# Softplus as one ScalarE function in a fused Mamba and feed-forward layer, its second half beside the silus of z

## The reference

```python
xi, z = split(x @ W_in.T)                       # 512 channels each
u  = silu(causal_conv4(xi) + conv_b)
dbl = u @ W_xproj.T                             # 16 ranks of dt, then B (16) and C (16)
dt = softplus(dbl[:, :16] @ W_dt.T + b_dt)      # what the change is about
h_t = exp(dt_t * A) * h_{t-1} + (dt_t * u_t) * B_t     # 512 channels x 16 states
y  = (h_t . C_t + u * D_skip) * silu(z)
x1 = layernorm(x + y @ W_out.T)
out = layernorm(x1 + (silu(x1 @ wg.T) * (x1 @ wu.T)) @ wd.T)
```

## Time and profile before

| | |
|---|---|
| median of 3 runs | 1799.51 us (1798.69 to 1802.62) |
| span of the profiled execution | 1797.7 us; the page gives no other time for it, and the median of the runs lies 1.8 us above this span |
| busy, share of the span | PE 96%, ACT 95%, DVE 93%, POOL 82% |
| granted TensorE clock, mean | 0.992 of full speed |
| DMA, share of 16 engines | under 20% |

### The profile page before, as it was taken

How to read it: one execution, slowest core, us unless ns; L and a number is a source line. 1 busy time by engine, 2 the same in 40 slices (tenths; PEclk the granted TensorE clock), 3 DMA queues, 4 the chain that set the end, 5 groups by cost and what they waited for, 6 DMA issues and landing times.

```text
span 1797.7 us, 40378 instructions
## 1 busy us (share of the span) xinstructions
PE 1734.7 (96%) x15678; PEld 1214.6 (68%) x15678; DVE 1675.1 (93%) x1970; ACT 1712.9 (95%) x2907; POOL 1477.8 (82%) x852
## 2 busy tenths in 40 slices
PE   7779999999999999999999999999999999999997
PEld 3456676767667676676767667676676767667676
DVE  5999999999999999999999999999999999999974
ACT  6999999999999999999999999999999999999971
POOL 5897987979889797997979889797987979889850
PEclk9999999999999999999999999999999999999999
DMA  7040211304013030211304013040311304022000
GB/s 211 1 121 1 56 65 15 118 11 121 3 16 118 15 118 2 66 68 16 118 10 123 2 15 119 14 119 1 74 60 16 118 13 121 1 39 83 1 25 24
DMA packets 171487, 100.57 MB, mean 56 GB/s; under 512 B 139408, under 2 KB 157584, under 8 KB 163232
## 3 DMA queue, kind: packets, MB, share of 16 engines
q1 hardware_dynamic: 171296, 97.98, 19.3%
HBM read 88.52 MB, written 9.44 MB: 54 GB/s over the span
## 4 chain that ended last, share of the span: by engine, by line
PE 48%; ACT 26%; DVE 11%; issue 9%; POOL 5%; SPq 0%; DMA 0%; ACTq 0%; POOLq 0%; DVEq 0%
PE ring L1162 17%; PE tp L1141 13%; ACT decay L706 8%; ACT hT L713 7%; PE yb L1155 7%; DVE h L917 6%; POOL drive L568 4%; PE ring L1254 3%; PE ring L1230 3%; DVE acc L938 3%; PE ring L1199 2%; ACT L743 1%; ACT acc L722 1%; PE ring L1220 1%; ACT dt L760 1%
## 5 line engine op out<-in xcount | busy, mean ns | idle before, releaser
L568 POOL TENSOR_TENSOR drive<-dtu,b_all 128x1024 f32<-128x1024 f32 x511 | 1204.4, 2389 | 17.6 <-DVE acc L938 9.2
L706 ACT ACTIVATE decay<-dt,a_neg 128x512 f32<-128x512 f32 x1024 | 705.0, 717 | 7.2 <-DVE h L917 6.4
L917 DVE TENSOR_TENSOR_SCAN h<-decay,h,drive 128x512 f32<-128x512 f32 x512 | 620.5, 1267 | 9.4 <-ACT decay L706 6.4
L1141 PEld LDWEIGHTS tp<-ident,h 128*128 128x128 f32 x4096 | 463.9, 141 | 240.1 <-issue 124.1
L917 DVE TENSOR_TENSOR_SCAN h<-decay,drive 128x512 f32<-128x512 f32 x512 | 592.3, 1208 | 29.2 <-ACT decay L706 25.3
L713 ACT ACTIVATE hT<-tp 128x512 f32<-128x512 f32 x1024 | 595.9, 618 | 11.8 <-PE tp L1141 10.9
L1141 PE MATMUL tp<-ident,h 128*128 128x128 f32 x4096 | 564.1, 277 | 37.9 <-ACT hT L713 29.1
L1155 PE MATMUL yb<-hT,diag_c 128*32 128x128 f32 x8192 | 275.8, 277 | 6.5 <-ACT yt L734 5.3
L1155 PEld LDWEIGHTS yb<-hT,diag_c 128*32 128x32 f32 x8192 | 210.7, 110 | 82.5 <-issue 48.8
L1162 PE MATMUL ring<-xt,w_in 128*128 128x512 f32 x512 | 245.2, 602 | 2.3 <-ACT acc L754 2.3
L1162 PE MATMUL ring<-xt,w_g 128*128 128x512 f32 x360 | 170.6, 596 | 0.0
(11 more groups left out here) (132 smaller groups left out, 1648.1 us busy)
## 6 DMA issues: line engine op xcount, KB each, us to landing
b_all<-bc_scratch SPq DMA_DIRECT2D x63, 1024.0 KB, 7.2
xt<-in_xT SPq DMA_DIRECT2D x16, 512.0 KB, 4.7
res<-in_x SPq DMA_DIRECT2D x16, 512.0 KB, 6.6
out<-res SPq DMA_DIRECT2D x15, 512.0 KB, 2.9
c_col<-bc_scratch SPq DMA_DIRECT2D x256, 2.0 KB, 2.4
bc_scratch<-dbl SPq DMA_DIRECT2D x16, 64.0 KB, 1.6
b_all<-bc_scratch SPq DMA_DIRECT2D x2, 512.0 KB, 4.4
w_g<-in_w_gT SPq DMA_DIRECT2D x1, 768.0 KB, 6.3
```

What stands on the lines that cost most here:

```text
L568: tt(drive[:, j % 4, :, :], src, b_all[:, n:n + 2, :], ALU.mult).then_inc(g_dr, 1)
L706: act(decay[decay_slot(k.parity, i)][:, :], dt[:, cb, :], ACT.Exp, scale=a_neg[:, cb, n:n + 1]).then_inc(a_da, 1)
L917: nc.vector.tensor_tensor_scan(h[:, h_slot(k.parity, q), at:at + T, i % 4], decay[decay_slot(k.parity, i)][:, :], drive[:, (i // 2) % 4, i ...
L1141: last = nc.tensor.transpose(tp[g % 2][:, b * P:(b + 1) * P], h[:, h_slot(k.parity, q), t0:t0 + TS, :].rearrange("p t s -> p (t s)"), iden ...
```

## The change

Exp, Ln and max become one ACTIVATE with the function Softplus, on ACT, and DVE has no part in it. The semaphores of the three steps (`a_e`, `a_ln`, `v_dt`) become one, `a_dt`, which ACT raises. A new wait on `g_dtu` guards the overwriting of `dt`. The written-out load of the Exp and Ln table goes; the builder places what loads the functions need. Half 0 keeps its place in steady chunks. Half 1 moves in the steady chunks from ACT's place (3, 1) to (4, 1), ahead of `sz 0` and `sz 1`; in the first and the last chunk it stays at (0, 0) and (2, 3).

```diff
-    (3, 1): [("log", 1)], (3, 2): [("hT", 8), ("hT", 9)], (3, 3): [("xi", 1)], (4, 1): [("sz", 0), ("sz", 1)],
+    (3, 2): [("hT", 8), ("hT", 9)], (3, 3): [("xi", 1)], (4, 1): [("log", 1), ("sz", 0), ("sz", 1)],
...
-    (5, 3): [("max", 1), ("norm", 0), ("conv", 0, 1), ("conv", 1, 0), ("conv", 1, 1), ("conv", 2, 0), ("conv", 2, 1), ("conv", 3, 0), ("conv", 3, 1)],
+    (5, 3): [("norm", 0), ("conv", 0, 1), ("conv", 1, 0), ("conv", 1, 1), ("conv", 2, 0), ("conv", 2, 1), ("conv", 3, 0), ("conv", 3, 1)],
...
-    (14, 0): [("r2", 0), ("skip", 2)], (14, 1): [("max", 0)], (15, 0): [("r2", 1)],
+    (14, 0): [("r2", 0), ("skip", 2)], (14, 1): [], (15, 0): [("r2", 1)],
...
-            def softplus_log(k, half):
+            def softplus(k, half):
 
                 two = dt[:, 2 * half:2 * half + 2, :]
                 wait(eng, a_xb, k.count(4, 2 * half + 2))
-                act(two, acc[:, 2 * half:2 * half + 2, :], ACT.Exp).then_inc(a_e, 1)
-                eng.wait_ge(a_e, k.count(2, half + 1))
-                act(two, two, ACT.Ln, bias=1.0).then_inc(a_ln, 1)
+                wait(eng, g_dtu, k.count(2, half + 1 - 2))
+                act(two, acc[:, 2 * half:2 * half + 2, :], ACT.Softplus).then_inc(a_dt, 1)
...
                 if what == "log" and i == 0 and head:
-                    nc.scalar.preload_act_table_set(EXP_LN_SET)
-                    softplus_log(k + 1, 0)
+                    softplus(k + 1, 0)
...
-            nc.scalar.preload_act_table_set(EXP_LN_SET)
             eng.wait_ge(l_w, ALL_LOADED)
             act(a_neg[:, :, :], a_neg[:, :, :], ACT.Exp).then_inc(a_set, 1)
             add_bias(k0, 0)
             add_bias(k0, 1)
-            for cb, (e, ln) in enumerate(((f_e, f_ln), (a_e, a_ln))):
+            for cb, done in enumerate((f_dt, a_dt)):
                 eng.wait_ge(a_xb, cb + 1)
-                act(dt[:, cb, :], acc[:, cb, :], ACT.Exp).then_inc(e, 1)
-                eng.wait_ge(e, 1)
-                act(dt[:, cb, :], dt[:, cb, :], ACT.Ln, bias=1.0).then_inc(ln, 1)
+                act(dt[:, cb, :], acc[:, cb, :], ACT.Softplus).then_inc(done, 1)
...
-            def softplus_max(k, half):
-
-
-                two = slice(2 * half, 2 * half + 2)
-                wait(eng, a_ln, k.count(2, half + 1))
-                stt(dt[:, two, :], dt[:, two, :], 40.0, acc[:, two, :], ALU.min, ALU.max).then_inc(v_dt, 1)
```

More of the change, by code:

```diff
@@ L38 @@
 STEPS = CB * N
-EXP_LN_SET = "natural_log_exp_and_others"
 SILU_SET = "silu_and_others"
@@ L124 @@
 DVE_FIRST = {
-    (2, 2): [("max", 1)], (3, 2): [("conv", 0, 0)],
+    (2, 2): [], (3, 2): [("conv", 0, 0)],
     (7, 0): [("conv", 0, 1), ("conv", 1, 0), ("conv", 1, 1), ("conv", 2, 0), ("conv", 2, 1), ("conv", 3, 0), ("conv", 3, 1)],
-    (10, 0): [("skip", 0)], (12, 3): [("skip", 1)], (13, 3): [("max", 0)],
+    (10, 0): [("skip", 0)], (12, 3): [("skip", 1)], (13, 3): [],
     (14, 2): [("skip", 2)],
@@ L178 @@
     (4, 1): [("norm", 0)], (5, 3): [("gs", 0)], (6, 1): [("gs", 1)],
-    (6, 2): [("gs", 2), ("max", 1), ("hid", 0)], (6, 3): [("skip", 0), ("hid", 1)], (8, 0): [("hid", 2)],
+    (6, 2): [("gs", 2),("hid", 0)], (6, 3): [("skip", 0), ("hid", 1)], (8, 0): [("hid", 2)],
     (8, 1): [("gs", 3)], (9, 3): [("gs", 4)], (10, 0): [("hid", 3)], (10, 2): [("gs", 5)],
@@ L416, in mamba_ffn @@
         a_da = sem("a_da"); a_ev = sem("a_ev"); a_xi = sem("a_xi"); a_u = sem("a_u"); a_z = sem("a_z")
-        a_sz = sem("a_sz"); a_xb = sem("a_xb"); a_dbl = sem("a_dbl"); a_e = sem("a_e"); a_ln = sem("a_ln")
+        a_sz = sem("a_sz"); a_xb = sem("a_xb"); a_dbl = sem("a_dbl"); a_dt = sem("a_dt")
         a_y = sem("a_y"); a_x1T = sem("a_x1T"); a_th = sem("a_th"); a_o = sem("a_o"); a_set = sem("a_set")
-        v_h = sem("v_h"); v_x1 = sem("v_x1"); v_y = sem("v_y"); v_conv = sem("v_conv"); v_dt = sem("v_dt")
+        v_h = sem("v_h"); v_x1 = sem("v_x1"); v_y = sem("v_y"); v_conv = sem("v_conv");
         v_r1 = sem("v_r1"); v_s1 = sem("v_s1"); v_gs = sem("v_gs")
@@ L430, in mamba_ffn @@
         e_n = sem("e_n"); e_var = sem("e_var"); e_std = sem("e_std"); e_o = sem("e_o")
-        f_e = sem("f_e"); f_ln = sem("f_ln"); f_dt = sem("f_dt"); f_dtu = sem("f_dtu"); f_diag = sem("f_diag"); f_conv = sem("f_conv"); f_b = sem("f_b"); f_dr = sem("f_dr")
+        f_dt = sem("f_dt"); f_dtu = sem("f_dtu"); f_diag = sem("f_diag"); f_conv = sem("f_conv"); f_b = sem("f_b"); f_dr = sem("f_dr")
         conv_loads = [
@@ L560, in drive_unit @@
                 if first and j == 4:
-                    eng.wait_ge(v_dt, 1)
+                    eng.wait_ge(a_dt, 1)
                     tt(dtu[:, 1, :], dt[:, 1, :], u[:, 0, 1, :], ALU.mult).then_inc(f_dtu, 1)
@@ L597, in dt_times_u @@
                 two = slice(2 * half, 2 * half + 2)
-                wait(eng, v_dt, k.count(2, half + 1))
+                wait(eng, a_dt, k.count(2, half + 1))
                 wait(eng, g_dr, k.count(32, -32 + 16 * (half + 1)))
@@ L704, in decay_step @@
                 elif i % 32 == 0 or first and i == N:
-                    wait(eng, v_dt, k.count(2, i // 32 + 1))
+                    wait(eng, a_dt, k.count(2, i // 32 + 1))
                 act(decay[decay_slot(k.parity, i)][:, :], dt[:, cb, :], ACT.Exp,
@@ L717, in copy_xi @@
                 wait(eng, g_head, k.count(1, 1))
-                wait(eng, v_dt, k.count(2, -1 + cb // 2))
+                wait(eng, a_dt, k.count(2, -1 + cb // 2))
                 if cb == 0:
@@ L801, in item @@
                 if what == "log" and i == 0 and head:
-                    nc.scalar.preload_act_table_set(EXP_LN_SET)
-                    softplus_log(k + 1, 0)
+                    softplus(k + 1, 0)
                 if what == "log" and i == 1:
-                    softplus_log(k, 1)
+                    softplus(k, 1)
                 if what == "y":
@@ L995, in item @@
                 i, *part = of or [None]
[L996 to L1000, removed]
                 if what == "conv" and head:
@@ L1035, in _ @@
             ts(a_neg[:, :, :], a_neg[:, :, :], -1.0, None, ALU.mult).then_inc(v_set, 1)
[L1036 to L1041, removed]
+            eng.wait_ge(f_dt, 1)
+            tt(dtu[:, 0, :], dt[:, 0, :], u[:, 0, 0, :], ALU.mult).then_inc(f_dtu, 1)
             for half in range(2):
```

## The result

The changed kernel takes 1846.11 us (median of 4, 1843.33 to 1847.37) against 1799.48 us: 1.0252 times as long, 95% interval 1.0238 to 1.0267. It is 46.6 us slower where 30.6 were forecast, and 4 us beyond the range of 1806 to 1842.

What follows compares the result with a forecast made beforehand. Each chunk was taken as about 21 us set by ACT from the burst at (4, 1), then about 87 us set by TensorE. 28 us for 14 chunks plus 2.3 at the ends, +30.6 unrounded, gave 1830 us, range 1806 to 1842.

Steps and rivals of the forecast that it cites:

- The operations: On ACT: Softplus takes 1.06 us and shares a table with neither Silu nor Exp (0.85); ten loads a chunk for eight.
- The burst at (4, 1): On ACT: one more load and Softplus add 2.38 us, 6.1 us in all; net 2.0 us a chunk, times 14 = 28.
- the 0.4 us: Ahead of (4, 1): of 2.15 us freed at (3, 1), ACT can win only 0.4 us, as scan 16 holds a decay.
- So I cost it at nothing: At (13, 3): half 0's block grows by 0.33 us of ACT, covered by TensorE's stretch; uncovered, 4.6 us in all.
- The maxes: On DVE: two maxes, 2.67 us a chunk, removed; time taken from DVE alone is worth little.
- The 87 us: Rest of each chunk up to the burst at (4, 1): about 87 us in which only TensorE's rate sets the end.
- TensorE's wait of 2 us: Behind the burst at (4, 1): PE waits about 2 us for hT L713, with no slack to take it.
- The ends: Last chunk +1.0 us, setup and first chunk +1.3 us; together +2.3 us.
- Absorbed but for the throughput: Rival, 0.14: stalls at (4, 1) are made good later, only ACT's added work counts; +10 us, 1810 us.
- VectorE's relief decides: Rival, 0.08, faster: the max's 1.2 us a chunk leaves the path; -14.5 us, 1785 us.
- Softplus shares Silu's table: Rival, 0.10: at (4, 1) Softplus adds 0.7 us a chunk and no load; +12 us, 1812 us.

Runs made afterwards that it cites:

- half 1 alone: Changed kernel with half 0 made by Exp and Ln again, without the max; half 1 stays Softplus at (4, 1): 1841.45 us, ratio 1.0229.
- Half 0 alone: Kernel before with only half 0 changed to Softplus at (13, 3); half 1 keeps Exp, Ln and max at (3, 1): 1801.45 us, ratio 1.0007.
- run 3: Changed kernel with 8 matmuls of a zero weight put into TensorE's wait behind the burst at (4, 1): 1834.15 us, ratio 1.0184.
- run 4: Kernel before with only half 1's Exp and Ln moved from (3, 1) to (4, 1), max kept, no load added: 1836.43 us, ratio 1.0203.
- run 8: Kernel before with VectorE's max left out in all places, Exp and Ln kept: 1796.70 us, ratio 0.9978.
- run 9: Changed kernel with copies hT 10 and hT 11 moved from behind the burst at (4, 1) to ahead of it: 1846.06 us, ratio 1.0256.
- run 2: Changed kernel with 60 matmuls of a zero 128x32 weight put into TensorE's wait ahead of transposes 12: 1985.19 us, ratio 1.1034.

## Why the prediction was right and wrong

**The operations: right.** Softplus took 1057 ns (1.06 forecast). It has a table of its own: ten loads a chunk for eight. The load costs 1.29 us from start to start in a row, so the drain of about 1380 ns that the Trainium skill's page "ScalarE: Activation LUTs", section "What ACT_TABLE_LOAD costs", adds to each did not show in the changed trace either.

**The burst at (4, 1): right in mechanism and size, but for the 0.4 us.** The burst is 6.13 us and TensorE and VectorE wait 2.12 us each. The term was 2.38 - 0.4 = 2.0 us a chunk. Measured from the two kernels that share the missing max, half 1 alone (undisturbed chunks, 109.83 in the mean) less no max (107.54), it is 2.29. The step "Only 0.4 us can be won" failed: less than 0.1 was. It looked at scan 16 alone. What holds ACT ahead of the burst is TensorE's product xi 1, then its two copies, then two decays, one behind the other without a gap from 714.77 us to 717.24. It was so before the change already: the copy began 0.08 us after the product's end, so no more than that could be won, and the rest of the freed time became ACT's waits of 1.35 and 0.49 us. This costs 14 x 0.3 = 4 us.

**"So I cost it at nothing": wrong.** Half 0's longer block at (13, 3) was priced at 0.33 us and held to be covered. The chunk with both halves and the clock held up (110.12) less half 1 alone undisturbed (109.83) is 0.29 us: paid nearly in full, 4 us. The maxes were costed at nothing too; without them a chunk is 0.31 us shorter, -4 us. That the two cancel is luck. Half 0 alone agrees (107.81 against 107.85), though only one of the two maxes is gone there. The 87 us that I took as TensorE's alone are thus a close race: that the chain of waits names TensorE from one end to the other does not say how far behind the second is. The chunk after the one in the earlier trace rows has a row that warns of it, and so has every second chunk of the kernel before:

```profile
889.34 1.14 PE L1141 MATMUL tp<-ident,h 128*128 128x128 f32 x8 [0.61 <-ACT hT L713]
```

**What was missing: TensorE's clock.** The prediction named TensorE's wait of 2 us and gave it no price beyond itself, although the windows showed a granted clock of 1.00 over the steady part, in which TensorE's wait at this place was 0.35 us. Without the half clock a chunk is 110.12 us, with it 110.87: 0.75 us a chunk, 14 x 0.75 = 10.5 us, and 12 us between the medians of the changed kernel and run 3. Of the missed terms this is the largest, and without it the result lies in the range (run 3: 1834.15). The Trainium skill, page "TensorE: Matmul & The Clock Gate", section "What's actually happening", says that a gate lets the full clock through according to how busy the array has been, and that the throttled state is the default; the rows fit the first, 0.50 behind the wait, but in the seven other chunks the same wait left 1.00, and none of them shows what the default is. The wait should have stood as a rival with a range, as its price could not be read from the steady part before.

**The sum.** For 14 chunks: burst +2.29, half 0 +0.29, max -0.31, clock +0.75, together +3.02 us, as 110.87 - 107.85. They must add up, as each is the difference between one kernel and the next (before, no max, half 1 alone, run 3, changed). A check from outside these is the move alone: 2.05 us moved to (4, 1) cost 1.97 us a chunk with the clock undisturbed. The chunks are 42 of the 46.6 us. The ends were forecast at +2.3. The end behind the last of the 14 loads gave 0 where +1.0 stood, although the last chunk has the two loads more; whether it absorbs them, or the missing maxes and less half clock at the end (6.5 us for 9.3) pay for them, is not shown. The rest is some 4 us in the setup and the first chunk. There the trace shows ACT's first decays late by 2.9 us, 1.4 of them already before the first changed instruction, and more half clock, about 31 us for 21. How much of these 4 us is the change's is not settled, since the start moves by up to 3 us from one profile to the next.

**The rivals.** "Absorbed but for the throughput" is out by run 4, where ACT's sum did not change and 36 us came. "VectorE's relief decides" had the right sign and a quarter of the size (run 8). "Softplus shares Silu's table" is out by the count of loads.

## What to carry to other kernels

In a kernel balanced to 1%, a moved operation is priced by the cover at its new place, and the cover ends sharply: here the first 3.7 us away from the copies cost nothing that shows, and beyond them nearly each microsecond is one of time, while the place left empty gives back only a wait. Before moving work onto a place, follow every input of the instruction ahead of it (copies of products, not the scan alone), and if the move makes TensorE wait, price the clock behind the wait too.
When a function gets a table of its own, count the loads at each place where it stands, and ask what else shares its neighbourhood: one ACTIVATE of 1.06 us for two that took 2.1 us together was no saving with a load of 1.3 us more beside it.

## What the runs showed of the hardware

- A wait of TensorE of 2.1 us, with one of 0.4 us a microsecond behind it, brought the half clock in 7 of 14 chunks of the changed kernel and in 5 of 14 of half 1 alone; one of 2.8 us in 7 of 14 (run 9), one of 1.8 us in 5 of 14 (run 4), waits of 0.9 us and less in none. Equal waits thus bring it in some chunks and not in others, and what decides is not shown. Each fall made the way from the silus to the table load ahead of u 1.5 to 1.6 us longer. Eight matmuls that compute nothing, put into the wait, saved 12 us of 1846.
- A 128x32 weight with 128 columns takes 0.11 us a pass when pass follows pass in one block of 32 partitions, and 0.03 us in the sum, where four blocks take turns (run 2). Nothing was run to part the blocks from the other differences of the two groups.
